# Down projections of a mixture-of-experts block as seven block products per expert

## The reference, cut to what matters

```python
h = concat([cls_tok, patches(x) @ W.T + b + pos])                 # 64 x 197 x 256
q, k, v = split(layernorm(h) @ w_qkv.T)                           # 16 heads of 16
a = q @ k.T / 4;  a = a - max(a)                                  # per head and row
p = s(a) / sum(s(a))     # s is a cubic in a for a >= 0, the inverse of a cubic for a < 0
h = h + (p @ v) @ w_out.T + b_out
t = layernorm(h)
u = sigmoid(t @ Wu + bu);  kk = clip(ceil(4 * u), 1, 4)           # per row
y[e] = relu(t @ W1[e] + b1[e]) @ W2[e] + b2[e]                    # e = 0..3, 256 -> 1024 -> 256
out = h + sum over i = 1..4 of where(kk >= i, u / i, 0) * y[(row + i - 1) % 4]
```

## Time and profile before

| | |
|---|---|
| median of 3 runs | 4319.41 us (4319.26 to 4319.63) |
| profiled execution | 4319.93 us, of which the span is 4318.1 us |
| mean granted TensorE clock | 0.99 |
| TensorE busy | 4250.9 us (98%), 21312 matmul instructions |
| VectorE / ScalarE / GpSimd busy | 2289.0 (53%) / 2178.8 (50%) / 139.2 us (3%) |
| bytes moved by DMA | 65.62 MB, 15 GB/s on average |

### The profile page before, as it was taken

How to read it: one execution, slowest core, us unless ns; L and a number is a source line. 1 busy time by engine, 2 the same in 40 slices (tenths; PEclk the granted TensorE clock), 3 DMA queues, 4 the chain that set the end, 5 groups by cost and what they waited for, 6 DMA issues and landing times.

```text
span 4318.1 us, 54053 instructions
## 1 busy us (share of the span) xinstructions
PE 4250.9 (98%) x21312; PEld 2340.6 (54%) x21312; DVE 2289.0 (53%) x3334; ACT 2178.8 (50%) x2945; POOL 139.2 (3%) x141
## 2 busy tenths in 40 slices
PE   6799999999999999999999999999999999999999
PEld 3455555555555555555555555555555555555555
DVE  4555555555555555555555555555555555555542
ACT  4444555445555445554455554455544555544552
POOL 1000000000000000000000000000000000000000
PEclk8899999999999999999999999999999999999999
DMA  3000000000000000000000000000000000000000
GB/s 130 12 3 14 16 16 3 16 14 16 16 3 16 16 14 16 16 3 16 14 16 16 3 16 16 14 16 16 3 16 14 16 16 3 16 16 14 5 5 8
DMA packets 29992, 65.62 MB, mean 15 GB/s; under 512 B 5360, under 2 KB 20400, under 8 KB 28720
## 3 DMA queue, kind: packets, MB, share of 16 engines
q1 hardware_dynamic: 26720, 62.07, 4.3%
q10 hardware_dynamic: 3024, 0.09, 0.0%
HBM read 49.24 MB, written 12.91 MB: 14 GB/s over the span
## 4 chain that ended last, share of the span: by engine, by line
PE 97%; DVE 1%; ACT 1%; issue 1%; POOL 0%; DMA 0%; DVEq 0%; SPq 0%; ACTq 0%; POOLq 0%
PE ps L716 33%; PE ps L727 32%; PE ps L785 6%; PE ps L751 5%; PE ps L739 5%; PE ps L767 4%; PE ps L824 4%; PE ps L833 3%; PE ps L841 2%; PE ps L699 1%; PE ps L798 1%; PE ps L816 1%; PE ps L810 1%; PE ps L792 0%; PE ps L804 0%
## 5 line engine op out<-in xcount | busy, mean ns | idle before, releaser
L716 PE MATMUL ps<-xn,w1s 128*128 128x394 f32 x4096 | 1563.0, 505 | 0.1
L727 PE MATMUL ps<-hT,w2s 128*128 128x394 f32 x4096 | 1534.8, 497 | 0.1
L428 ACT ACTIVATE hT<-ps,b1s 128x394 f32<-128x394 f32 x1024 | 604.3, 590 | 1342.1 <-PE ps L716 1338.0
L716 PEld LDWEIGHTS ps<-xn,w1s 128*128 128x128 f32 x4096 | 743.6, 190 | 619.7 <-issue 170.7
L727 PEld LDWEIGHTS ps<-hT,w2s 128*128 128x128 f32 x4096 | 758.5, 189 | 564.2 <-issue 36.8
L499 DVE SCALAR_TENSOR_TENSOR probs<-probs,ps 99x788 f32<-99x788 f32 x512 | 484.0, 972 | 728.9 <-ACT probs L332 728.9
L568 DVE TENSOR_REDUCE lows<-ps 99x8 f32<-99x1576 f32 x256 | 459.9, 1798 | 507.0 <-PE ps L751 506.9
L337 ACT ACTIVATE probs<-probs 99x1576 f32<-99x1576 f32 x256 | 388.7, 1518 | 194.4 <-DVE probs L499 194.4
L332 ACT ACTIVATE probs<-ps 99x788 f32<-99x788 f32 x512 | 394.7, 823 | 148.2 <-PE ps L739 146.4
L341 ACT ACTIVATE probs<-probs 99x1576 f32<-99x1576 f32 x256 | 386.6, 1510 | 0.1
L785 PE MATMUL ps<-x,wtok 128*128 128x392 f32 x744 | 257.1, 493 | 0.0
(11 more groups left out here) (82 smaller groups left out, 2464.3 us busy)
## 6 DMA issues: line engine op xcount, KB each, us to landing
x<-in_xT SPq DMA_DIRECT2D x31, 1188.0 KB, 5.8
out_rows<-rows SPq DMA_DIRECT2D x64, 99.0 KB
out_rows<-rows SPq DMA_DIRECT2D x64, 98.0 KB
w1s<-in_w SPq DMA_DIRECT2D x4, 1024.0 KB, 13.3
w2s<-in_w SPq DMA_DIRECT2D x4, 1024.0 KB, 15.3
x<-in_xT SPq DMA_DIRECT2D x6, 198.0 KB, 4.5
wtok<-in_w_tok SPq DMA_DIRECT2D x6, 128.0 KB, 3.9
wqk<-in_w_qk SPq DMA_DIRECT2D x1, 512.0 KB, 6.1
```

What stands on the lines that cost most here:

```text
L428: nc.scalar.activation(hT[:, j % 4, :], ps[:, U0 + up_turn(j) % 2, 0:N], ACT.Relu, bias=b1s[:, j // FB, j % FB:j % FB + 1]).then_inc(relu_ ...
L716: ins = mm(ps[:, U0 + up_turn(j) % 2, 0:N], w1s[:, e, kk, f * P:(f + 1) * P], xn2[:, n % 2, kk, :], start=kk == 0, stop=kk == DK - 1)
L727: ins = mm(ps[:, Y0 + m, 0:N], w2s[:, e, f, m * P:(m + 1) * P], hT[:, j % 4, :], start=f == 0, stop=f == FB - 1)
```

## The change

The down projection of an expert is seen as a product of 2 x 2 blocks: the left factor is W2[e], cut into halves of its 1024 hidden rows and of its 256 results; the right one is the hidden activations, cut into halves of the hidden numbers and into the two images. Seven block products (Strassen's scheme in Winograd's form) give the four blocks of the result. `product(x, k)` is product k of expert x (x counts experts over all pairs): 4 matmuls of 128 x 128 weights and 197 columns. The four sums of weights that it needs are made once at the start by GpSimd (`weight_sums`) from W2, which is loaded into `hT`'s space for that; three plain blocks of W2 are loaded again for each expert (`load_a`). The sums of hidden blocks are made by GpSimd for each couple of hidden blocks (`hidden_sums`, 3 instructions, 16 couples per pair); the sums of products by VectorE (`after_a` to `after_d`) into `c1` and `yw`. `y_weighted` reads `yw` instead of PSUM.

Products of an expert run behind the ups of the next expert: `experts(1)` is one up and, in seven of eight places, one product; the last expert of a pair runs in the next step. `to_rows` of an image pair moves from before gap 3 to after gap 7 for its first image, and `project_v`, `lowest` and the projections of queries and keys are in another order. The up weights are no longer kept: `w1s` has four places, refilled from HBM by SyncE (`load_w1`, two DMAs of 128 KB per couple).

`q` and `k_own` are gone: `q_of` and `k_of` write `q_max` and `k_one` directly, per image, and `lowest` uses these, 16 instructions of 197 columns in place of 8 of 394. `project` makes 197 columns at a time. `base_of` and `one_of` are gone. `gates` is split: its inverse stays behind block 1 (`sigmoid`), the rest goes behind blocks 5 and 6. `normal_rows2` and `gate_sum` move behind the sixth and before the seventh reduction.

```diff
-        w1s = sb("w1s", [P, E, DK, F])
-        w2s = sb("w2s", [P, E, FB, D])
+        w1s = sb("w1s", [P, 4, DK, 2 * P])
+        w_s = sb("w_s", [P, E, 4, FB // 2, P])
+        w_a = sb("w_a", [P, 3, FB // 2, P])
...
+            def load_w1(n, c):
+
+                wait(sp, up_done, at(n, UNITS, 2 * c - 6))
+                for k in range(DK):
+                    sp.dma_start(w1s[:, c % 4, k].rearrange("p (h x) -> p h x", h=2),
+                                 w1[c // 4][:, k, :].rearrange("p (h g x) -> p g h x", h=2, g=COUPLES)[:, c % 4]).then_inc(w1_in[c % 4], 16)
+
+            def load_a(x, i):
+
+                wait(sp, prod_done, at(x - 1, PRODUCTS, (1, 3, 7)[i]))
+                f, m = ((0, 0), (1, 0), (1, 1))[i]
+                sp.dma_start(w_a[:, i], w2[x % E][:, f * COUPLES:(f + 1) * COUPLES, m * P:(m + 1) * P]).then_inc(wa_in[i], 16)
...
+            def hidden_sums(c):
+                b = hidden(c)
+                pool.wait_ge(relu_ready, 2 * c + 2)
+                if c >= RING:
+                    pool.wait_ge(prod_done, products_of(c - RING, 6))
+                nc.gpsimd.tensor_tensor(t13(c), b[:, :, 1, :], b[:, 0], ALU.subtract).then_inc(t_ready, 1)
+                pool.wait_ge(t_ready, 3 * c + 1)
+                nc.gpsimd.tensor_tensor(b[:, 0, 1, :], b[:, 1, 1, :], t13(c)[:, 0, :], ALU.subtract).then_inc(t_ready, 1)
+                pool.wait_ge(t_ready, 3 * c + 2)
+                if c >= RING4:
+                    pool.wait_ge(prod_done, products_of(c - RING4, 7))
+                nc.gpsimd.tensor_tensor(t4(c), b[:, 0, 1, :], b[:, 1, 0, :], ALU.subtract).then_inc(t_ready, 1)
+
...
-            def q_of(f, o):
...
+            def q_of(f, o, img):
+
+                act.wait_ge(q_done, at(f, 4, 2 * img + o + 1))
+                wait(act, gap_done, at(f - 1, 8, 4 * img + 4))
+                for j in range(2):
+                    ins = nc.scalar.activation(q_max[:, o, j, img * S:(img + 1) * S], bank(f"q{o}{img}", f)[:, 0:S], ACT.Copy, scale=q_scale[:, 1 - j:2 - j])
+                ins.then_inc(q_ready, 1)
 
...
+            def k_of(f, o, img):
+
+                dve.wait_ge(k_done, at(f, 4, 2 * img + o + 1))
+                wait(dve, gap_done, at(f - 1, 8, 4 * img + 4))
                 for j in range(2):
-                    ins = nc.vector.tensor_scalar(k_own[:, o, j, :], bank(f"k{o}", f)[:, 0:N], head_mask[:, 1 - j:2 - j], None, ALU.mult)
+                    ins = nc.vector.tensor_scalar(k_one[:, o, j, img * S:(img + 1) * S], bank(f"k{o}{img}", f)[:, 0:S], head_mask[:, 1 - j:2 - j],
+                                                  spare[:, j:j + 1], ALU.mult, ALU.add)
                 ins.then_inc(k_ready, 1)
...
+            def after_a(x):
+
+                dve.wait_ge(prod_done, at(x, PRODUCTS, 2))
+                wait(dve, c_ready, x)
+                wait(dve, b_ready, at(x, 2, -1))
+                nc.vector.tensor_copy(c1[:, 0], ps[:, Y0, 0:S]).then_inc(a_ready, 1)
+                dve.wait_ge(a_ready, at(x, 2, 1))
+                nc.vector.tensor_tensor(c1[:, 1], ps[:, Y0, S:N], c1[:, 0], ALU.add).then_inc(a_ready, 1)
+
+            def after_c(x):
+
+                dve.wait_ge(prod_done, at(x, PRODUCTS, 4))
+                dve.wait_ge(a_ready, at(x, 2, 2))
+                wait(dve, y_ready, at(x, 2, -1))
+                nc.vector.tensor_tensor(two(yw[:, 0]), two(ps[:, Y1, 0:N]), c1[:], ALU.add).then_inc(c_ready, 1)
+
+            def after_b(x):
+
+                dve.wait_ge(prod_done, at(x, PRODUCTS, 6))
+                wait(dve, y_ready, at(x, 2, 0))
+                nc.vector.tensor_tensor(two(yw[:, 1]), ps[:, Y0, S:N].unsqueeze(1).broadcast_to((P, 2, S)), c1[:, 1:2].broadcast_to((P, 2, S)),
+                                        ALU.add).then_inc(b_ready, 1)
+                dve.wait_ge(b_ready, at(x, 2, 1))
+                dve.wait_ge(c_ready, at(x, 1, 1))
+                nc.vector.tensor_tensor(yw[:, :, S:N], ps[:, Y0, 0:S].unsqueeze(1).broadcast_to((P, DK, S)), yw[:, :, S:N], ALU.add).then_inc(b_ready, 1)
+
+            def after_d(x):
+
+                dve.wait_ge(prod_done, at(x, PRODUCTS, 7))
+                dve.wait_ge(b_ready, at(x, 2, 2))
+                nc.vector.tensor_tensor(yw[:, 1, 0:S], yw[:, 1, 0:S], ps[:, Y1, 0:S], ALU.subtract).then_inc(d_ready, 1)
+
+            def y_weighted(x, m):
+                if m == 0:
+                    dve.wait_ge(b_ready, at(x, 2, 2))
+                    dve.wait_ge(gate, at(x // E, 8, 8))
+                else:
+                    dve.wait_ge(d_ready, at(x, 1, 1))
+                nc.vector.scalar_tensor_tensor(out=two(yw[:, m, :]), in0=two(yw[:, m, :]), scalar=b2s[:, x % E, m:m + 1], in1=weight_of(x % E),
+                                               op0=ALU.add, op1=ALU.mult).then_inc(yw_ready, 1)
+
...
+                def early(s):
+
+                    x = (n * E + s // 4) - 1
+                    if s % 4 == 0 and (has_n and x >= 1 or s == 0 and has_t):
+                        after_d(x - 1)
+                        y_weighted(x - 1, 1)
...
+                    if has_n and x >= 0 or s < 4 and has_t:
+                        if s % 4 == 1:
+                            after_a(x)
+                        if s % 4 == 2:
+                            after_c(x)
+                        if s % 4 == 3:
+                            after_b(x)
+
+                def late(s):
+                    x = (n * E + s // 4) - 1
+                    if s % 4 == 0 and (has_n and x >= 1 or s in (0, 4) and has_t):
+                        y_added(x - 1, 1)
+                    if s % 4 == 3 and (has_n and x >= 0 or s < 4 and has_t):
+                        y_weighted(x, 0)
+                        y_added(x, 0)
...
                 for k in range(8):
-                    if k == 4 and has_n:
-                        y_weighted(n, 0)
+                    early(k)
                     if has_b:
                         poly(b, k, 0)
...
                     if k == 4 and has_f:
                         spread(f, "var", var_done, vt_ready)
+                    late(k)
+                    if k == 1 and has_n:
+                        sigmoid(n)
                     if k == 6 and has_n:
-                        y_added(n, 0)
-                    if k == 1 and has_n:
-                        gates(n)
+                        gates(n, (2, 3))
                     if k == 2 and has_f:
                         centre(f)
                     if k == 4 and has_f:
                         normal_rows(f)
-                    if k in (6, 7) and has_f:
-                        k_of(f, k - 6)
+                    if k in (5, 6) and has_f:
+                        k_of(f, k - 5, 0)
+                    if k == 6 and f == 0:
+                        k_of(f, 0, 1)
+                        k_of(f, 1, 1)
                     if k in (3, 5, 7) and has_b:
                         normal(b, (k - 3) // 2)
+                    if k == 5 and has_n:
+                        gates(n, (0, 1))
                 for k in range(8):
-                    if k in (0, 4) and has_n:
-                        y_weighted(n, k // 4 + 1)
+                    if k < 6 and k != 3:
+                        early(8 + k)
+                    if k == 7 and has_b:
+                        gate_sum(b)
                     if has_f:
                         low(f, k)
                     if k == 1 and has_b:
                         whole(b, 3)
-                    if k in (0, 4) and has_n:
-                        y_added(n, k // 4 + 1)
+                    if k in (0, 1) and has_f and has_b:
+                        k_of(f, k, 1)
+                    if k == 3:
+                        early(11)
+                    elif k < 7:
+                        late(8 + k)
                     if k == 1 and has_b:
                         normal(b, 3)
                     if k == 3 and has_b:
                         h2_of(b, 0)
                         h2_of(b, 1)
+                    if k == 3:
+                        late(11)
...
                     if k == 5 and has_b:
                         spread(b, "var2", var2_done, vt2_ready)
+                    if k == 6 and has_b:
                         normal_rows2(b)
-                    if k == 6 and has_b:
-                        gate_sum(b)
+                    if k >= 6:
+                        early(8 + k)
                     if k == 7 and has_b:
                         zb_of(b)
                     if k == 7 and has_f:
                         q_max_of(f, 1)
+                    if k == 7:
+                        late(15)
 
...
-            def down(n, j):
...
+            def product(x, k):
+
+                first, last = x * COUPLES, x * COUPLES + COUPLES - 1
+                if k == 0:
+                    if x == 0:
+                        pe.wait_ge(q_max_ready, at(1, 4, 4))
+                        pe.wait_ge(ws_ready, 4 * E)
+                    wait(pe, b_ready, at(x, 2, 0))
```

(44 more changed lines are left out.)

409 lines of the change are left out of this document (226 added, 183 removed).

## The result

The changed kernel takes 4254.85 us, the median of 4 runs (4254.53 to 4257.48); the kernel before, run beside it, takes 4319.34 us (4317.22 to 4319.63). The ratio is 0.9853, with a 95% interval of 0.9836 to 0.9870. The forecast was 4222 with a range of 4160 to 4300. So the direction and the range held, and the point was 33 us too low: of 158 us that the column count promised, 65 arrived.

What follows compares the result with a forecast made beforehand. Columns through TensorE were taken as the bound. From 4319.9 us, 158 saved on columns left 4162; one-off costs made it 4168, and 54 of TensorE waiting for VectorE 4222; range 4160 to 4300.

Steps and rivals of the forecast that it cites:

- Prices on TensorE: A 197-column matmul costs 167 ns with its weight load hidden; net saving 4.93 us a pair, 158 us in all.
- Rival C: Weight loads on TensorE do not overlap each other and set a 190 ns pace: 4411 us, chance 0.04.
- VectorE's load: Sums and copies of products, 3.1 us per expert, plus keys: VectorE's 71.65 us a pair becomes 85, no bound as a mean.
- First place: Blocks 5 to 7: gap block 7 waits for VectorE's keys, 0.8 to 1.9 us late, 0.2 without GpSimd.
- Second place: End of the pair: the transposes wait for VectorE's last reduction, 1.0 to 1.5 us late through couple 14's GpSimd sums.
- The low ends: Lowest lateness of the two VectorE places, 0.8 + 1.0 = 1.8 us in each of 30 pairs: 54 us.
- bare period: Time of one image pair in the middle with no TensorE waits: 127 us.
- Beginning: Prologue: GpSimd's weight sums, about 20 us, and fewer ScalarE copies change the time by -5 to +5, taken as 0.
- First pair and tail: Pair 1's first eight slots lack products, costing 5 us in waits; seven products (9.4 us) and a 1.2 us wait end the kernel.
- A: Rival: VectorE's and GpSimd's added work all fits into gaps and TensorE never waits: 4168 us, chance 0.26.
- B: Rival: every VectorE instruction waits for GpSimd, PSUM-input polynomials too, 8.5 us a pair: 4423 us, chance 0.08.
- D: Rival: streamed weights arrive late, perhaps 1 us in each of 16 loads: 4700 us, chance 0.02.

Runs made afterwards that it cites:

- ninth run: The sixth run with the gates of ranks 0 and 1 moved to block 4, ahead of the first normalisation: 4163.43 us, ratio 0.9642.
- tenth run: The ninth run with the gates of ranks 0 and 1 left behind block 5, as in the changed kernel: 4167.06 us, ratio 0.9651.
- sixth run: Changed kernel with keys first, end-of-pair reorder, late weight sums, gates (0, 1) behind the sigmoid, ScalarE's invert and v_of earlier; part of result altered: 4164.78 us.

## Why the prediction was right, and by what it missed

**Prices on TensorE: right.** 167 ns a product, 4.93 us a pair, weight loads hidden; the ninth run's 126.82 stands beside 131.97 - 4.93 = 127.04. Rival C is refuted: with 166 ns in the median and 32 of 6277 starts above 185, loads do not set the pace.

**VectorE's load: right in sum, 86.8 for 85.** The evictions of an expert cost 2.75 us (357, 364, 548, 561, 568 and 351 ns) instead of 3.1; the contention that I had not put into that sum (3.6 us: 86.8 less the 83.2 with small sums) made up for it, so that the agreement is luck. GpSimd came out at 43.75 instead of 37, since its sums take 1.17, 0.67 and 0.64 us on average instead of 1.03 and twice 0.55: they wait for VectorE too (the shortest are 0.94, 0.53 and 0.54).

**First place: right.** The wait is where it was forecast, at the keys, 1.40 us where the range was 0.8 to 1.9. Its two parts were right as well: 0.2 without GpSimd (0.23 in the run with small sums), the rest with it.

**Second place: the size nearly right, the place wrong.** I forecast 1.0 to 1.5 at the transposes and got 0.77 at the product. The step that failed is that I followed only the chain from normalisation to reduction, and did not ask what else is queued behind the normalisation on VectorE: `after_c`, which a product wants earlier than the transposes want the reduction. Once TensorE has lost 0.77 there, the transposes are late by nothing.

**The low ends: the step that missed most.** I took 0.8 + 1.0 = 1.8 us a pair, because TensorE "waits only for what remains after each margin". Reading the two sums again, the margins were already in them, so that the low ends took them off twice. The measured waits at the two places make 2.2, and 0.7 came from the small places, for which I had kept 0 to 0.6 in the range and nothing in the sum (the mean product 0.43, the queries 0.17, the first lowest block 0.12). Of these I had named only the lowest block. The largest, at the mean product, is the wait at a polynomial's bank that I had given as a sign of being wrong; it came from ScalarE's order, on which I had said that ScalarE is late nowhere. The bare period was 0.2 us shorter than forecast. Together the period was 129.69 instead of 128.84: 0.85 x 30 = 25 us of the 33.

**Beginning: wrong, 8.6 us instead of 0.** Until the gates of the first pair, 155.0 us became 163.6 (both taken at the broadcast of the gate logits). Of these, 3.8 are there at the first gap block, from the layer norm beside the weight sums. I had looked at GpSimd's 20 us there as work that lies beside other work, and had seen a row in which a VectorE instruction stands for a GpSimd one, but did not use it at the one point of the kernel where VectorE's layer norm is on the critical path. The runs with the late weight sums give 3.2 to 4.4 back at that block. The other 4.9 us arise behind gap block 7 of the first pair: to the gate logits it is 53.0 us before and 58.0 after. The projections of the second image (16 instructions) now lie in that stretch, and its mean granted clock is 0.65 where it was 0.67; the late sums do not change it (58.0 in the ninth and tenth run). How much of it is order and how much the clock was not tried.

**First pair and tail.** From the first pair's gates to the second's, 132.78 us became 127.69, 5.1 less, where 4.93 + 9.4 - 5 - 1.8 = 7.5 less was forecast; without the period's 0.85 that is 1.6 lost, so the slots without products cost 6.6 instead of 5. From the gates of the last pair but one to the end it went down by 2.4, where 2 x 4.93 - 9.4 - 1.2 would have it up by 0.7: 3 better. So 8.6 + 25 + 1.6 - 3 = 32 of the 33, where the first and the third number are those of one trace and good to 2 or 3 us only.

**The rivals.** A (all of it hides) was not what this kernel did, with 2.9 us a pair of waits, but it is what the order could do: 4163 against its 4168. B is refuted by the polynomials' 970 ns and by the run with small sums: even without most of the contention only 55 us come back, where B needed 255. D is refuted by the run with small streams and by a list of waits in which TensorE waits for no DMA once the pairs run.

**Still open.** Why the first pair loses 6.6 and not 5, if it does, was not tried by itself, nor what makes the 4.9 us behind its gap block 7. Nor was each of the later edits of the sixth run alone, save the place of gates (0, 1). Together they give 22.4 us: 0.72 a pair (127.541 to 126.823), 21.5, and gates of the first pair that come 3.7 us earlier (169.7 to 166.0), of which the ends take 2.8 back, where was not looked into.

## What to carry to other kernels

When a change loads an engine that works in order, the mean load (87 of 130 us) says little; go through its program at each place where TensorE takes something from it and ask of each instruction ahead whether anybody waits for it. If not, it goes behind the eviction: moving two instructions past six gave 42 us here, and all the orders together 91. Contention between engines has no price of its own. It is a length added to certain instructions (here sums and products with both inputs in SBUF, and scalings from SBUF to SBUF, beside a GpSimd sum), to be put into that same walk with the whole length of the neighbour, above all where a chain has no other work behind it, as in a prologue. And where an instruction can be chosen to stand beside the sum, it is better one that reads PSUM.

## What the runs showed of the hardware

- A VectorE sum or product of two SBUF tensors and a GpSimd sum that it meets do not run side by side; the later one ends only after the earlier: 0.57 became 1.41 to 1.51 us beside sums of 512 elements, 0.98 became 1.92 there and 1.61 beside one of 394. GpSimd pays too: its 394-element sum has a shortest time of 0.94 us and a mean of 1.17. That a scaling with one SBUF input (363 to 445 ns on average, up to 0.59) is among them I had not expected.
- The second normalisation meets a 394-element sum in 31 of 32 pairs. In the 30 where the sum was first it takes 1.61 us, in the one where it was first itself 0.98.
- An instruction with one PSUM input is not touched (970 and 568 ns), nor did ScalarE need more time. Nor is the reciprocal from SBUF to SBUF (1391 ns in the 65 of 128 that lie beside a GpSimd sum), nor the shuffle (L618, 372 to 375 ns, 64 of 128 beside one).
- In the first 160 us of all these traces the granted clock moves between 1.2 and 2.4 GHz (0.65 to 0.69 on average between gap block 7 and the gates of the first pair), and the same instructions there take 54.3 to 58.0 us from run to run.
- Float32 matmuls of 197 columns with new 128x128 weights each start every 167 ns, 394 columns every 331: the load stays hidden at half the length.
- 70 GB/s in pieces of 512 bytes, beside a TensorE that is busy for 97% of the span, cost nothing against 18 GB/s in as many pieces: 4254.85 against 4253.86 us.
